# A graph network's recurrent kernel: tiles 4 to 7 prepared every four units with their state split in two pieces, masking moved to GpSimd, last chain in halves

## Chip, cores and metric

The kernel runs on one core of a Trainium2 chip. The metric is the device time of one execution in microseconds; lower is better.

## What is computed

```python
h = relu(layernorm(x))                       # x: 64 graphs, 128 nodes, 128 channels
A = (adj != 0)
for l in range(5):
    m   = einsum('bnd,de->bne', h, weight[l])
    agg = einsum('bij,bid->bjd', A, m)
    # GRU cell:
    gi, gh = agg @ w_ih.T + b_ih, h @ w_hh.T + b_hh
    r, z = sigmoid(i_r + h_r), sigmoid(i_z + h_z)
    n = tanh(i_n + r * h_n)
    h = (1 - z) * n + z * h
return x + h * mask[..., None]
```

## The kernel before

The 64 graphs make 16 tiles of four graphs, 128 channels by 512 node columns. The tiles go in four groups of four. Within a group the five layers run one after another, and within a layer the four tiles. A pair (tile, layer) is a **unit**; there are N = 80, numbered K = 0 to 79: tiles 0 to 3 have units 0 to 19, tiles 4 to 7 units 20 to 39, and so on, so unit K + 4 is the next layer of unit K's tile. Every product is made of three float16 matmuls from high and low halves (`three`, L293 to L295).

**One unit.** TensorE makes three products from the old state, `ps_r`, `ps_z`, `ps_hn` (`h_products`), then two from the aggregated state s, then the `aggregate` of the *next* unit into `ps_s` (eight narrow matmuls, L366 and L367), then `ps_in` from s. ScalarE makes r (L478), z (L484), the high half of s (L472), the high half of the previous unit's state (`state_high`, L494) and n (L488). VectorE makes r * hn (L624), the input of tanh (L630), the low half of s of the next unit (`s_low`, L618), and the new state in two steps (L636, L641). GpSimd makes z * h (`kept`, L816) and the low half of the previous unit's state (`state_low`, L821). SyncE then issues `transpose(K)` (L242), a DMA that turns both halves into `nat`; `aggregate(K + 4)` waits for it.

**Preparation.** Each tile from 4 on passes through stages beside the units of earlier tiles. `prep[t]` is the unit of stage 0, set in L54 to L57 by counting back from the tile's first unit with a distance of 3 units (tiles 4 to 7) or 5. Stage 0: loads of adj and x on SyncE, `moments` on VectorE. Stage 1: `aggregate` of the moments on VectorE, `inverse_std` on GpSimd. Stages 3 and 4: `layernorm` in halves on ScalarE (L442). Stage 5: `natural_high` (ScalarE) and `natural_low` (GpSimd, L804). Stage 6: `split` on ScalarE (L467), then two DMA transposes, `transpose_first` and `transpose_halves`; for tiles below 8 also `adjacency` on GpSimd (L800). Stage 7: `adjacency` on VectorE (L609) for the later tiles. Stages 8 and 9: `join` in halves on VectorE (L676). `STAGES` is their number.

**Results.** A finished tile is masked (`masked_result`, L827) in the unit `ends[t]`, added to x (`final`, L835) in the next, and stored by SyncE in the one after (`storing`). `fetching` says when `load_ends` brings the x and mask rows of a tile, six units ahead of `ends`; the mask row is broadcast to 128 partitions. In the last group, units 76 to 78, VectorE multiplies by the mask itself (`masked_state`, L648). The last unit has a chain of its own: `masked_open`, `last_result`.

**What sets the order.** Each engine runs a loop over K with the calls written out by hand, and takes them strictly in that order; so does SyncE with its DMA issues, all on one queue. In SyncE's loop, iteration K has `transpose(K - 1)`, the loads of stage 0, the transposes of stage 6, the store and the fetch, in this order.

```python
prep[t] = min(at[t, 0] - STAGES, prep[t + 1] - gap if t + 1 < TILES else N)
ends[t] += (prep[TILES - 1] + 3 - ends[t]) % SPREAD
```

Of the kernel before, what the change touches and what calls it, by code (L numbers as in the profile page):

```python
# [27 lines left out]
FINISH = 3  # L28
STAGES = 10
# [7 lines left out]
def gnn_kernel(nc, x, xT, adj, mask_row, fold_lhs, w_ihT, w_hhT, bias_ih, bias_hh, ident, out):  # L37
# [10 lines left out]
    END = at[starts[-1], LAST]  # L48
# [33 lines left out]
    with ExitStack() as ctx:  # L82
# [66 lines left out]
        ps_s, ps_t, ps_f = bank("ps_s"), bank("ps_t"), bank("ps_f")  # L149

# [31 lines left out]
        def block_of(tile_ap, q):  # L182
            return tile_ap[:, q * P:(q + 1) * P]

# [30 lines left out]
        def _(sp):  # L215
# [16 lines left out]
            def transpose_halves(t):  # L232
                sp.wait_ge(split_done, t - FIRST + 1)
# [39 lines left out]
            for K in range(1, N + 2):  # L273
# [6 lines left out]
                if K in tile_at_stage[6]:  # L280
                    transpose_first(tile_at_stage[6][K])
                    transpose_halves(tile_at_stage[6][K])
                if K in storing:
                    store(storing[K])
                for t in fetching.get(K, ()):
                    load_ends(t)
            for f in range(FRING):
                sp.wait_ge(stored[f], 16 * len(range(f, TILES, FRING)))
# [146 lines left out]
        def _(act):  # L435
# [26 lines left out]
            def split(t):  # L462

                act.wait_ge(h0_done, 2 * t + 2)
                if t - FIRST >= 2:
                    act.wait_ge(halves_loaded[t % 2], 16 * ((t - FIRST) // 2))
                nc.scalar.copy(halves[:, t % 2], h0[:, t % LN].bitcast(U16).rearrange("p (c b) -> p b c", b=2)).then_inc(  # L467
                    split_done, 1)
# [11 lines left out]
            def gate_z(K):  # L480
# [3 lines left out]
                nc.scalar.activation(z[:, K % 2], ps_z[:], ACT.Sigmoid, bias=b_sum[:, 1:2], scale=unscale[:, 0:1]).then_inc(z_done, 1)  # L484

# [14 lines left out]
            def move_mask():  # L500
# [3 lines left out]
                act.wait_ge(s_lo_done, N)  # L504
                nc.scalar.copy(ps_s[:], mask_in[:, f]).then_inc(mask_moved, 1)

            def store_last():
                t = TILES - 1
                act.wait_ge(last_out, 1)
                act.dma_start(out_t[t], x_out[:, t % FRING]).then_inc(stored[t % FRING], 16)  # L510
# [30 lines left out]
            for K in range(N):  # L541
# [16 lines left out]
                if K == 0:  # L558
                    layernorm(3, 0)
                    layernorm(3, 1)  # L560
                else:
                    gate_n(K)
# [19 lines left out]
        def _(dve):  # L582
# [67 lines left out]
            def masked_open(K):  # L650
# [5 lines left out]
                nc.vector.scalar_tensor_tensor(out=mask_in[:, f], in0=z[:, K % 2], scalar=1.0, in1=ps_s[:],  # L656
                                               op0=ALU.subtract, op1=ALU.mult).then_inc(open_done, 1)

            def last_result(K):

                f = units[K][0] % FRING
                dve.wait_ge(n_done, K + 1)
                dve.wait_ge(open_done, 1)
                nc.vector.tensor_tensor(ps_in[K % 2][:], mask_in[:, f], ps_in[K % 2][:], ALU.mult).then_inc(zn_done, 1)
                dve.wait_ge(zn_done, K + 1)
                dve.wait_ge(last_kept, 1)
                nc.vector.tensor_tensor(x_out[:, f], x_out[:, f], ps_in[K % 2][:], ALU.subtract).then_inc(last_out, 1)
# [79 lines left out]
            for K in range(N):  # L747
# [8 lines left out]
                if K in tile_at_stage[0]:  # L756
                    moments(tile_at_stage[0][K])
# [164 lines left out]
```

## Time and profile before

| | |
|---|---|
| time, median of 3 runs | 371.98 us (371.85 to 372.28) |
| the profiled execution's own time | 371.11 us |
| its span, first to last instruction | 369.2 us |
| TensorE matmul | 360.0 us busy, 98% |
| VectorE | 322.8 us, 87% |
| ScalarE | 299.8 us, 81% |
| GpSimd | 263.6 us, 71% |
| mean granted TensorE clock | 0.997 of 2.4 GHz |
| packets of SyncE's DMA queue | 45.37 MB, 55.3% of the time of 16 DMA engines |
| chain of work that ended last | TensorE 90%, VectorE 4%, DMA 2%, GpSimd 2% |

The page's busy shares are averages. The timeline of an engine gives each instruction's start, its length and, in brackets, how long the engine had been idle and for whom. Durations of neighbours overlap by about 0.1 us, since an engine begins an instruction before its predecessor has fully ended.

### The profile page before, as it was taken

The numbers are of one execution on the slowest core, as the hardware profiler recorded it, in microseconds if no ns is written. First come the engines' busy times: TensorE is split into PE (matmuls) and PEld (weight loads), VectorE is DVE, ScalarE is ACT, GpSimd is POOL, SyncE is SP. The second block draws the span as 40 slices with busy tenths as digits, with TensorE's granted clock in tenths as the row PEclk, the third lists the DMA queues.
The fourth block names the chain that finished last, engine by engine and source line by source line (L and its number), as shares of the span: only waits on it lengthen the run. The fifth ranks groups of instructions, "written<-read, shape, count | busy, mean of one in ns | idle before, by whom it ended". The sixth has DMA issues, their size and how long they took to land.

```text
span 369.2 us, 6528 instructions
## 1 busy us (share of the span) xinstructions
PE 360.0 (98%) x2125; PEld 181.1 (49%) x2125; DVE 322.8 (87%) x588; ACT 299.8 (81%) x495; POOL 263.6 (71%) x261
## 2 busy tenths in 40 slices
PE   7999999999999999999999999999999999999992
PEld 3455555544454555555545455555545555555541
DVE  4977898899889999999999999999998988787886
ACT  5997788998879988888877889899877767777753
POOL 3765758889578878787656878888756777755574
PEclk9999999999999999999999999999999999999998
DMA  8634443857662693939624384756834543349522
GB/s 245 211 59 86 115 97 76 170 126 151 152 115 45 147 180 78 228 68 200 169 42 105 64 197 85 164 123 158 151 94 112 130 99 59 89 100 231 124 57 85
DMA packets 108512, 46.03 MB, mean 125 GB/s; under 512 B 97728, under 2 KB 98112, under 8 KB 108480
## 3 DMA queue, kind: packets, MB, share of 16 engines
q1 hardware_dynamic: 108336, 45.37, 55.3%
q8 instruction: 17, 0.28, 0.3%
q10 hardware_dynamic: 144, 0.26, 0.2%
q14 instruction: 15, 0.12, 0.1%
HBM read 17.57 MB, written 4.19 MB: 59 GB/s over the span
## 4 chain that ended last, share of the span: by engine, by line
PE 90%; DVE 4%; DMA 2%; POOL 2%; issue 1%; ACT 1%; DVEq 0%; POOLq 0%
PE ps_r L293 9%; PE ps_z L294 9%; PE ps_z L293 9%; PE ps_r L294 9%; PE ps_z L295 9%; PE ps_r L295 9%; PE ps_s L366 5%; PE ps_s L367 5%; PE ps_in L295 4%; PE ps_hn L294 4%; PE ps_in L293 4%; PE ps_in L294 4%; PE ps_hn L295 4%; PE ps_hn L293 4%; DMA hp<-nat 1%
## 5 line engine op out<-in xcount | busy, mean ns | idle before, releaser
L816 POOL TENSOR_TENSOR zh<-z,h 128x512 f32<-128x512 f32 x80 | 101.9, 1273 | 81.4 <-ACT z L484 81.3
L478 ACT ACTIVATE r<-ps_r,b_sum,unscale 128x512 f32<-128x512 f32 x80 | 62.2, 778 | 37.9 <-PE ps_r L295 37.5
L488 ACT ACTIVATE ps_in<-ps_in,b_ih,unscale 128x512 f32<-128x512 f32 x80 | 60.1, 751 | 22.3 <-DVE ps_in L630 21.3
L821 POOL TENSOR_TENSOR hp<-h,hp 128x512 f16<-128x512 f32 x64 | 74.1, 1157 | 0.0
L624 DVE SCALAR_TENSOR_TENSOR rhn<-ps_hn,b_hn,r 128x512 f32<-128x512 f32 x80 | 59.8, 748 | 10.3 <-ACT r L478 9.8
L630 DVE TENSOR_TENSOR ps_in<-ps_in,rhn 128x512 f32<-128x512 f32 x80 | 56.0, 700 | 11.5 <-PE ps_in L295 6.7
L484 ACT ACTIVATE z<-ps_z,b_sum,unscale 128x512 f32<-128x512 f32 x80 | 61.6, 770 | 0.7 <-PE ps_z L295 0.7
L641 DVE TENSOR_TENSOR h<-zh,ps_in 128x512 f32<-128x512 f32 x76 | 52.2, 687 | 8.5 <-DVE ps_in L636 0.5
L636 DVE SCALAR_TENSOR_TENSOR ps_in<-z,ps_in 128x512 f32<-128x512 f32 x79 | 54.7, 692 | 5.6 <-ACT ps_in L488 5.6
L618 DVE TENSOR_TENSOR s_lo<-ps_s,s_hi 128x512 f16<-128x512 f32 x80 | 54.4, 680 | 0.4 <-ACT s_hi L472 0.4
L472 ACT CAST s_hi<-ps_s 128x512 f16<-128x512 f32 x80 | 46.6, 583 | 0.0
L366 PE MATMUL ps_s<-a,nat 128*128 128x128 f16 x320 | 44.3, 219 | 0.0
L367 PE MATMUL ps_s<-a,nat 128*128 128x128 f16 x320 | 44.3, 219 | 0.0
L494 ACT CAST hp<-h 128x512 f16<-128x512 f32 x64 | 40.7, 635 | 0.1
L366 PEld LDWEIGHTS ps_s<-a,nat 128*128 128x128 f16 x320 | 31.3, 98 | 9.4 <-POOL nat L804 0.4
L367 PEld LDWEIGHTS ps_s<-a,nat 128*128 128x128 f16 x320 | 31.3, 98 | 9.0
L293 PE MATMUL ps_z<-s_hi,v_hi 128*128 128x512 f16 x80 | 30.3, 379 | 0.5 <-DVE s_lo L618 0.5
L293 PE MATMUL ps_r<-s_hi,v_hi 128*128 128x512 f16 x80 | 30.4, 380 | 0.2 <-DVE s_lo L618 0.2
L293 PE MATMUL ps_r<-hp,u_hi 128*128 128x512 f16 x79 | 30.0, 379 | 0.5 <-DMA hp<-nat 0.2
L294 PE MATMUL ps_r<-s_lo,v_hi 128*128 128x512 f16 x80 | 30.3, 379 | 0.0
L295 PE MATMUL ps_r<-s_hi,v_lo 128*128 128x512 f16 x80 | 30.3, 379 | 0.0
L294 PE MATMUL ps_z<-s_lo,v_hi 128*128 128x512 f16 x80 | 30.3, 379 | 0.0
(115 smaller groups left out, 745.0 us busy)
## 6 DMA issues: line engine op xcount, KB each, us to landing
x_in<-in_x SPq DMA_DIRECT2D x16, 256.0 KB, 3.8
adj_in<-in_adj SPq DMA_DIRECT2D x16, 256.0 KB, 3.4
x_out<-in_xT SPq DMA_DIRECT2D x16, 256.0 KB, 3.1
mask_in<-in_mask_row SPq DMA_DIRECT2D x16, 256.0 KB, 3.8
out<-x_out SPq DMA_DIRECT2D x15, 256.0 KB, 2.7
nat<-hp SPq DMA_TRANSPOSE x64, 3.1
fold_in<-in_fold_lhs SPq DMA_DIRECT2D x1, 320.0 KB, 3.9
out<-x_out ACTq DMA_DIRECT2D x1, 256.0 KB, 2.1
```

The source lines that it names most:

```text
L293: nc.tensor.matmul(ps[:], w_hi, m_hi, start=start, stop=False)
L294: nc.tensor.matmul(ps[:], w_hi, m_lo, start=False, stop=False)
L295: return nc.tensor.matmul(ps[:], w_lo, m_hi, start=False, stop=stop)
L366: nc.tensor.matmul(block_of(ps_s, q), block_of(nat_hi(t), q), a_q, start=True, stop=False)
L367: last = nc.tensor.matmul(block_of(ps_s, q), block_of(nat_lo(t), q), a_q, start=False, stop=True)
L478: nc.scalar.activation(r[:], ps_r[:], ACT.Sigmoid, bias=b_sum[:, 0:1], scale=unscale[:, 0:1]).then_inc(r_done, 1)
L484: nc.scalar.activation(z[:, K % 2], ps_z[:], ACT.Sigmoid, bias=b_sum[:, 1:2], scale=unscale[:, 0:1]).then_inc(z_done, 1)
L488: nc.scalar.activation(ps_in[K % 2][:], ps_in[K % 2][:], ACT.Tanh, bias=b_ih[:, 2:3], scale=unscale[:, 0:1]).then_inc(n_done, 1)
L624: nc.vector.scalar_tensor_tensor(out=rhn[:], in0=ps_hn[:], scalar=b_hn[:, 0:1], in1=r[:], op0=ALU.add, op1=ALU.mult).then_inc(rhn_done, 1)
L630: nc.vector.tensor_tensor(ps_in[K % 2][:], ps_in[K % 2][:], rhn[:], ALU.add).then_inc(npre_done, 1)
L816: nc.gpsimd.tensor_tensor(zh[:, K % 2], z[:, K % 2], h[:, t % RING], ALU.mult).then_inc(zh_done, 1)
L821: nc.gpsimd.tensor_tensor(h_lo(t), h[:, t % RING], h_hi(t), ALU.subtract).then_inc(h_lo_done, 1)
```

## The change

Five things are changed.

- Tiles 4 to 7 follow each other by four units and not three. `prep` becomes 2, 6, 10, 14 for tiles 4 to 7 (it was 4, 7, 10, 13) and 19, 24, ... 54 for tiles 8 to 15 (it was 18, 23, ... 53).
- There are nine stages. `layernorm` stands in stages 2 and 3, `natural_high`, `natural_low` and the first half of `split` in 4, its second half, the two transposes and GpSimd's `adjacency` in 5, VectorE's `adjacency` in 6, `join` in 7 and 8. `moments` of tiles 4 to 7 come two units ahead of stage 0.
- Since `ends` is aligned to `prep`, the stores move too: from units 23, 28, ... 58 to 19, 24, ... 59, and the fetches from 15, 20, ... 50 to 11, 16, ... 51; `load_ends(9)` falls in unit 54.
- `END` is 78: units 76 and 77 write their state like all others, and GpSimd masks it ahead of the next unit's `kept`. The last tile's old state is masked one unit earlier, and its mask is copied to PSUM ahead of the last z.
- In unit 79, tanh and the two operations behind it run in halves of 256 columns, and each half is stored by itself, the first by SyncE, the second by ScalarE's queue.

The core of the diff:

```diff
-FINISH = 3
-STAGES = 10
+FINISH = 4
+STAGES = 9
...
-    END = at[starts[-1], LAST]
+    END = N - 1 - 1
...
-        gap = 3 if t < starts[1] + GROUPS[1] else SPREAD
+        gap = 4 if t < starts[2] else SPREAD
...
+    measured = {prep[t] - (2 if t < starts[2] else 0): t for t in prep}
...
+        last_n = (ps_f, ps_s)
...
-                if K in tile_at_stage[6]:
-                    transpose_first(tile_at_stage[6][K])
-                    transpose_halves(tile_at_stage[6][K])
+                if K in tile_at_stage[5]:
+                    transpose_first(tile_at_stage[5][K])
+                    transpose_halves(tile_at_stage[5][K])
...
+            sp.wait_ge(last_out, 1)
+            sp.dma_start(half_of(out_t[TILES - 1], 0), half_of(x_out[:, (TILES - 1) % FRING], 0)).then_inc(
+                stored[(TILES - 1) % FRING], 16)
...
-            def split(t):
-
-                act.wait_ge(h0_done, 2 * t + 2)
+            def split(t, half):
+
+                act.wait_ge(h0_done, 2 * t + 1 + half)
...
+            def last_gate_n(K, half):
+                act.wait_ge(npre_done, K + 1)
+                nc.scalar.activation(last_n[half][:, 0:TILE // 2], half_of(ps_in[K % 2], half), ACT.Tanh, bias=b_ih[:, 2:3],
+                                     scale=unscale[:, 0:1]).then_inc(n_done, 1)
...
                 else:
+                    move_mask()
                     gate_z(K)
                     gate_r(K)
-                    move_mask()
...
+                if K in tile_at_stage[2]:
+                    layernorm(tile_at_stage[2][K], 0)
                 if K in tile_at_stage[3]:
-                    layernorm(tile_at_stage[3][K], 0)
+                    layernorm(tile_at_stage[3][K], 1)
                 if K in tile_at_stage[4]:
-                    layernorm(tile_at_stage[4][K], 1)
+                    natural_high(tile_at_stage[4][K])
+                if K in tile_at_stage[4]:
+                    split(tile_at_stage[4][K], 0)
                 if K in tile_at_stage[5]:
-                    natural_high(tile_at_stage[5][K])
-                if K in tile_at_stage[6]:
-                    split(tile_at_stage[6][K])
+                    split(tile_at_stage[5][K], 1)
...
-                if K in tile_at_stage[0]:
-                    moments(tile_at_stage[0][K])
+                if K in measured:
+                    moments(measured[K])
...
                     masked_open(K)
-                    last_result(K)
+                    last_open_n(K, 0)
+                    last_open_n(K, 1)
+                    last_result(K, 0)
+                    last_result(K, 1)
...
             for K in range(N):
+                if END > K - 1 >= at[starts[-1], LAST]:
+                    masked_result(units[K - 1][0])
                 kept(K)
...
-                if K in tile_at_stage[5]:
-                    natural_low(tile_at_stage[5][K])
-                if K in tile_at_stage[6] and pool_compares(tile_at_stage[6][K]):
-                    adjacency(tile_at_stage[6][K])
+                if K in tile_at_stage[4]:
+                    natural_low(tile_at_stage[4][K])
+                if K in tile_at_stage[5] and pool_compares(tile_at_stage[5][K]):
+                    adjacency(tile_at_stage[5][K])
```

SyncE's queue around units 23 to 25, before. `nat<-hp` is a unit's state transpose, `hp<-nat` and `halves_t<-halves` are the transposes of a tile in preparation, `out_0<-x_out` is a store; the last two rows are a fetch.

```order
43 L242 DMA_TRANSPOSE nat<-hp 128x8x128 x3
44 L224 DMA adj_in<-in_adj 128x512
45 L219 DMA x_in<-in_x 128x512
46 L253 DMA out_0<-x_out 128x512
47 L242 DMA_TRANSPOSE nat<-hp 128x8x128
48 L230 DMA_TRANSPOSE hp<-nat 128x8x128
49 L236 DMA_TRANSPOSE halves_t<-halves 128x8x128
50 L242 DMA_TRANSPOSE nat<-hp 128x8x128
51 L248 DMA x_out<-in_xT 128x512
52 L249 DMA mask_in<-in_mask_row 128x512
```

The same place after the change.

```order
49 L248 DMA_TRANSPOSE nat<-hp 128x8x128 x3
50 L230 DMA adj_in<-in_adj 128x512
51 L225 DMA x_in<-in_x 128x512
52 L236 DMA_TRANSPOSE hp<-nat 128x8x128
53 L242 DMA_TRANSPOSE halves_t<-halves 128x8x128
54 L259 DMA out_0<-x_out 128x512
55 L248 DMA_TRANSPOSE nat<-hp 128x8x128 x2
56 L254 DMA x_out<-in_xT 128x512
57 L255 DMA mask_in<-in_mask_row 128x512
```

The loads, the two preparing transposes and the store stand between two neighbouring state transposes, where a state transpose used to divide them into two turns. The fetch has moved back by one.

GpSimd's last operations before, from the last `state_low` on (`L841` masks the last tile's old state, `L835` adds, `L847` is the last tile's share of z * h).

```order
252 L821 TENSOR_TENSOR hp<-h,hp 128x512
253 L816 TENSOR_TENSOR zh<-z,h 128x512
254 L841 TENSOR_TENSOR h<-mask_in,h 128x512
255 L835 TENSOR_TENSOR x_out<-x_out,mask_in 128x512
256 L816 TENSOR_TENSOR zh<-z,h 128x512
257 L835 TENSOR_TENSOR x_out<-x_out,mask_in 128x512
258 L816 TENSOR_TENSOR zh<-z,h 128x512
259 L847 TENSOR_TENSOR x_out<-x_out,zh 128x512
260 L835 TENSOR_TENSOR x_out<-x_out,mask_in 128x512
```

And after; `L854` is the masking that has come from VectorE.

```order
253 L848 TENSOR_TENSOR hp<-h,hp 128x512
254 L868 TENSOR_TENSOR h<-mask_in,h 128x512
255 L854 TENSOR_TENSOR mask_in<-mask_in,h 128x512
256 L843 TENSOR_TENSOR zh<-z,h 128x512
257 L862 TENSOR_TENSOR x_out<-x_out,mask_in 128x512
258 L854 TENSOR_TENSOR mask_in<-mask_in,h 128x512
259 L843 TENSOR_TENSOR zh<-z,h 128x512
260 L862 TENSOR_TENSOR x_out<-x_out,mask_in 128x512
261 L843 TENSOR_TENSOR zh<-z,h 128x512
262 L874 TENSOR_TENSOR x_out<-x_out,zh 128x512
263 L862 TENSOR_TENSOR x_out<-x_out,mask_in 128x512
```

The masking of the last old state comes ahead of unit 77's `zh`, and each of the two new maskings stands in front of a `zh`.

## Rows read from the trace of the kernel before

**Rows 1.** The page: engines; DMA issues with median us to landing.
```profile
PE 360.0 (98%) x2125; PEld 181.1 (49%) x2125; DVE 322.8 (87%) x588; ACT 299.8 (81%) x495; POOL 263.6 (71%) x261
...
nat<-hp SPq DMA_TRANSPOSE x64, 3.1
```

**Rows 2.** Timeline, GpSimd, unit 25: start us, us, engine, line, operation, out<-in.
```profile
129.87 1.16 POOL L821 TENSOR_TENSOR hp<-h,hp 128x512 f16<-128x512 f32 x1
```

**Rows 3.** Timeline, TensorE: the first matmul of two neighbouring aggregations.
```profile
131.89 0.22 PE L366 MATMUL ps_s<-a,nat 128*128 128x128 f16 x1
...
136.22 0.22 PE L366 MATMUL ps_s<-a,nat 128*128 128x128 f16 x1
```

**Rows 4.** Timeline, ScalarE: a split.
```profile
78.43 1.03 ACT L467 COPY halves<-h 128x1024 uint16<-128x1024 uint16 x1
```

**Rows 5.** Timeline, TensorE's weight loads; brackets: idle before, released by.
```profile
80.26 0.10 PEld L293 LDWEIGHTS ps_r<-hp,u_hi 128*128 128x128 f16 x1 [0.59 <-issue]
...
82.40 0.10 PEld L293 LDWEIGHTS ps_r<-s_hi,v_hi 128*128 128x128 f16 x1 [0.51 <-DVE s_lo L618]
```

**Rows 6.** Timeline, VectorE: an aggregate, a join, and an adjacency.
```profile
104.31 0.37 DVE L597 BATCH_NORM_AGGREGATE mean_var<-bn 128x2 f32<-128x6 f32 x4
104.60 0.42 DVE L676 COPY h<-halves_t 128x512 uint16<-128x512 uint16 x1
...
130.06 1.25 DVE L609 TENSOR_SCALAR a<-adj_in 128x512 f16<-128x512 f32 x1
```

**Rows 7.** Timeline, GpSimd: an adjacency, then natural_low and the next zh.
```profile
77.99 1.93 POOL L800 TENSOR_SCALAR a<-adj_in 128x512 f16<-128x512 f32 x1
...
122.60 1.16 POOL L804 TENSOR_TENSOR nat<-h,nat 128x512 f16<-128x512 f32 x1 [0.24 <-ACT nat L450]
124.31 1.27 POOL L816 TENSOR_TENSOR zh<-z,h 128x512 f32<-128x512 f32 x1 [0.54 <-ACT z L484]
```

**Rows 8.** Timeline, SyncE's queue: the issue of unit 23's transpose.
```profile
126.73 1.30 SPq L242 DMA_TRANSPOSE nat<-hp  x1
```

**Rows 9.** Timeline, SyncE's queue from 79.3 us: issues.
```profile
79.33 0.58 SPq L224 DMA_DIRECT2D adj_in<-in_adj  x1
79.95 0.43 SPq L219 DMA_DIRECT2D x_in<-in_x  x1
...
83.43 1.78 SPq L242 DMA_TRANSPOSE nat<-hp  x1
```

**Rows 10.** DMA issues from 79.3 to 83.6 us: us from issue to landing.
```profile
adj_in<-in_adj SPq DMA_DIRECT2D x1, 256.0 KB, 3.1
x_in<-in_x SPq DMA_DIRECT2D x1, 256.0 KB, 3.4
...
nat<-hp SPq DMA_TRANSPOSE x1, 3.7
```

**Rows 11.** Timeline, SyncE's queue from 254.2 us: issues.
```profile
254.26 0.44 SPq L253 DMA_DIRECT2D out<-x_out  x1
254.75 0.44 SPq L248 DMA_DIRECT2D x_out<-in_xT  x1
255.23 0.50 SPq L249 DMA_DIRECT2D mask_in<-in_mask_row  x1
```

**Rows 12.** DMA issues from 254.2 to 255.6 us: us from issue to landing.
```profile
out<-x_out SPq DMA_DIRECT2D x1, 256.0 KB, 3.4
x_out<-in_xT SPq DMA_DIRECT2D x1, 256.0 KB, 3.6
mask_in<-in_mask_row SPq DMA_DIRECT2D x1, 256.0 KB, 4.8
```

**Rows 13.** Timeline near the end: masking, the last unit's first s-product, last operations.
```profile
357.51 0.69 DVE L648 TENSOR_TENSOR mask_in<-mask_in,ps_in 128x512 f32<-128x512 f32 x1
...
360.31 0.39 PE L293 MATMUL ps_z<-s_hi,v_hi 128*128 128x512 f16 x1 [0.53 <-DVE s_lo L618]
...
365.05 0.69 DVE L664 TENSOR_TENSOR ps_in<-mask_in,ps_in 128x512 f32<-128x512 f32 x1 [0.23 <-ACT ps_in L488]
```

More of the change, by code:

```diff
@@ L183, in block_of, with half_of @@
             return tile_ap[:, q * P:(q + 1) * P]
+        def half_of(tile_ap, half):
+            return tile_ap[:, half * TILE // 2:(half + 1) * TILE // 2]
         def h_hi(t):
@@ L460, in transposed @@
                 nc.scalar.activation(h[:, t % RING], ps_t[:], ACT.Relu).then_inc(h_init, 1)
-            def split(t):
-                act.wait_ge(h0_done, 2 * t + 2)
+            def split(t, half):
+                act.wait_ge(h0_done, 2 * t + 1 + half)
                 if t - FIRST >= 2:
                     act.wait_ge(halves_loaded[t % 2], 16 * ((t - FIRST) // 2))
-                nc.scalar.copy(halves[:, t % 2], h0[:, t % LN].bitcast(U16).rearrange("p (c b) -> p b c", b=2)).then_inc(
-                    split_done, 1)
+                nc.scalar.copy(halves[:, t % 2, :, half * TILE // 2:(half + 1) * TILE // 2],
+                               h0[:, t % LN, half * TILE // 2:(half + 1) * TILE // 2].bitcast(U16).rearrange(
+                                   "p (c b) -> p b c", b=2)).then_inc(split_done, 1)
             def s_high(K):
@@ L503, in move_mask @@
                 act.wait_ge(ends_loaded[f], 32 * ((TILES - 1) // FRING + 1))
-                act.wait_ge(s_lo_done, N)
-                nc.scalar.copy(ps_s[:], mask_in[:, f]).then_inc(mask_moved, 1)
+                nc.scalar.copy(ps_t[:], mask_in[:, f]).then_inc(mask_moved, 1)
             def store_last():
                 t = TILES - 1
-                act.wait_ge(last_out, 1)
-                act.dma_start(out_t[t], x_out[:, t % FRING]).then_inc(stored[t % FRING], 16)
+                act.wait_ge(last_out, 2)
+                act.dma_start(half_of(out_t[t], 1), half_of(x_out[:, t % FRING], 1)).then_inc(stored[t % FRING], 16)
             def squares(weights, begin, sums):
@@ L655, in masked_open, with last_open_n, last_result @@
                 dve.wait_ge(mask_moved, 1)
-                nc.vector.scalar_tensor_tensor(out=mask_in[:, f], in0=z[:, K % 2], scalar=1.0, in1=ps_s[:],
+                nc.vector.scalar_tensor_tensor(out=mask_in[:, f], in0=z[:, K % 2], scalar=1.0, in1=ps_t[:],
                                                op0=ALU.subtract, op1=ALU.mult).then_inc(open_done, 1)
-            def last_result(K):
-                f = units[K][0] % FRING
-                dve.wait_ge(n_done, K + 1)
+            def last_open_n(K, half):
+                dve.wait_ge(n_done, K + 1 + half)
                 dve.wait_ge(open_done, 1)
-                nc.vector.tensor_tensor(ps_in[K % 2][:], mask_in[:, f], ps_in[K % 2][:], ALU.mult).then_inc(zn_done, 1)
-                dve.wait_ge(zn_done, K + 1)
+                n = last_n[half][:, 0:TILE // 2]
+                nc.vector.tensor_tensor(n, half_of(mask_in[:, units[K][0] % FRING], half), n, ALU.mult).then_inc(zn_done, 1)
+            def last_result(K, half):
+                dve.wait_ge(zn_done, K + 1 + half)
                 dve.wait_ge(last_kept, 1)
-                nc.vector.tensor_tensor(x_out[:, f], x_out[:, f], ps_in[K % 2][:], ALU.subtract).then_inc(last_out, 1)
+                result = half_of(x_out[:, units[K][0] % FRING], half)
+                nc.vector.tensor_tensor(result, result, last_n[half][:, 0:TILE // 2], ALU.subtract).then_inc(last_out, 1)
             def join(t, half):
@@ L755, in _ @@
                     adjacency(3)
-                if K in tile_at_stage[0]:
-                    moments(tile_at_stage[0][K])
+                if K in measured:
+                    moments(measured[K])
                 if K in tile_at_stage[1]:
                     aggregate(tile_at_stage[1][K])
-                if K in tile_at_stage[7] and not pool_compares(tile_at_stage[7][K]):
-                    adjacency(tile_at_stage[7][K])
+                if K in tile_at_stage[6] and not pool_compares(tile_at_stage[6][K]):
+                    adjacency(tile_at_stage[6][K])
                 for half in range(2):
-                    if K in tile_at_stage[8 + half]:
-                        join(tile_at_stage[8 + half][K], half)
+                    if K in tile_at_stage[7 + half]:
+                        join(tile_at_stage[7 + half][K], half)
                 if K == 0:
@@ L830, in final @@
                 f = t % FRING
-                if t < starts[-1]:
+                if at[t, LAST] < END:
                     pool.wait_ge(masked, t + 1)
                 else:
-                    pool.wait_ge(last_masked, t - starts[-1] + 1)
+                    pool.wait_ge(last_masked, at[t, LAST] - END + 1)
                 nc.gpsimd.tensor_tensor(x_out[:, f], x_out[:, f], mask_in[:, f], ALU.add).then_inc(out_done, 1)
```

9 lines of the change are left out of this document (6 added, 3 removed).

## The prediction

> **What bounds the kernel now.** I read the page's engine line first: TensorE is busy 360.0 of 369.2 us [rows 1]. A kernel like this gains only where TensorE's stream of matmuls has a hole, and loses only where a new hole opens. In the steady part the aggregations of neighbouring units start 4.33 us apart [rows 3], which is 18 wide matmuls and 8 narrow ones back to back. So the second view was the timeline of TensorE, searched for starts that follow their predecessor by more than the usual 0.22 us. From 27 to 359 us it found only a fold of weights, two pairs of short holes and one crumb, all before 97 us. The third view was the timeline of the other engines around these, the fourth the queue of DMA issues with the time to landing of each. From 97 to 359 us the stream has no hole. That stretch can't get faster; it can only be hurt.
>
> Where it could be hurt is read from slack. The state's `transpose` of a unit K is issued when GpSimd has written the low half (L821) in unit K+1, and its result is wanted by `aggregate(K+4)`. For K = 24 GpSimd ends at 129.87 + 1.16 = 131.03; the aggregation starts at 136.22 [rows 2, 3]. So **a transpose has 5.2 us from "ready" to "wanted"**. Undisturbed it lands 3.1 us after its issue [rows 1], and 2.1 us are spare.
>
> **Part 1: preparation of tiles 4 to 7, and the split in pieces.** Before, tiles 4 to 7 follow each other by three units, and a tile's `split` (stage 6) shares a unit with the next tile's first `layernorm` (stage 3). ScalarE then has a split of 1.03 us from 78.43 behind a half layernorm [rows 4], and the next r, whose sum was ready near 78.4, gets its turn when that is through, 0.9 us late. TensorE pays: the weights of the next unit are loaded after 0.59 us of idleness and those of its s-products after 0.51 us [rows 5]; start to start, the matmuls lose 0.29 and 0.18 us. The pair comes back three units later with 0.28 and 0.14, and one hole of 0.07 lies between. Sum: 0.96. With tiles four units apart and stages 2, 3, 4, 5 on ScalarE, no unit has two tiles' work; the fullest has `natural_high` and half a split. Half a split I take at 0.55, between 0.4 and 1.03 [rows 4]. That is 1.2 us where about 0.8 is free; r is 0.4 late, and the first hole needed r 0.9 late. Gain: **-1.0** (bounds -1.1 and -0.6, if VectorE's joins, up to 1.3 us in units 13 and 14, leave a crumb). The early `moments(4)` in unit 0 fills a wait of VectorE for `v_hi`; zero.
>
> Moments and aggregate of tiles 8 to 15 come one unit later. `aggregate` (0.37 us, of which 0.3 are its turn [rows 6]) now stands ahead of `adjacency` on VectorE in seven units (25, 30, ... 55). Added to a 1.25 us adjacency [rows 6] it would make s_lo 0.3 late, seven times. But a join lasted 0.42 us at 104.60, while GpSimd had only 4-column work, and the adjacency at 130.06 lasted 1.25 and ended at 131.31, 0.28 after GpSimd's L821 ended [rows 2, 6]. It is a wait, not work, and 0.3 more ahead of it disappears in it. I take 0, and keep 7 x 0.3 = 2.1 as a bound. The Trainium skill (SBUF — State Buffer, "Who interferes with whom") says the pair of ports that VectorE's two-port modes share with GpSimd is an exclusive lock for a whole instruction; by that rule the sum has 0 here, by adding durations 2.1.
>
> **Part 2: what moves on SyncE's queue.** This is the term that decides. Before, in each period of five units, loads and the store stand in one unit (23), `transpose_first` and `transpose_halves` in the next (24), the fetch in the third (25). After, stage 0 of one tile, stage 5 of the tile before and the store all fall on the same unit: 24, 29, 34, 39, 44, 49, 54. Between the transposes of units 23 and 24 then stand adjacency load, x load, two transposes and a store; before, only the two transposes. On top of that GpSimd has `natural_low` and `final` in one unit (23, 28, ...): natural_low ends near 123.75 [rows 7], final takes at least 1.27, as zh does, so the next zh starts at 125.0, not at 124.31, and the transpose of unit 23 is issued at 127.4, not at 126.73 [rows 7, 8].
>
> The price comes from the one place of before that has almost this queue, SyncE's turn from 79.33 us on: adjacency and x load, first, halves, state transpose. The adjacency load was issued at 79.33, the transpose at 83.43, and it landed 3.7 us later, at 87.13 [rows 9, 10]: **7.8 us after the adjacency load's issue**. In the new unit 24 that load is issued 1.3 after the transpose, at 128.7. The transpose of unit 24 would land at 136.5; with a store ahead of it too, later by one 256 KB copy. Landings lie 0.7 apart there (254.26 + 3.4 against 254.75 + 3.6) [rows 11, 12]. So 137.2 against 136.2: TensorE waits **1.0** in unit 27, likewise after units 29 and 34. Bounds: 0 (without the 0.7 of GpSimd and with the store free, 135.8) and 1.9 (issue at 133.3, landing 4.8, the longest shown [rows 12]).
> - Units 24, 29, 34: 3 x 1.0 = **+3.0** (0 to 5.7). Unit 39 is a last layer and has no transpose.
> - Units 44, 49: no x load, 0.9 less (79.33 + 3.1 against 79.95 + 3.4 [rows 9, 10]): 2 x 0.1 = **+0.2** (0 to 2.0).
> - Unit 54: `load_ends(9)` stands behind the store as well: 0.7 for x_out, and 1.7 for the mask row (254.75 + 3.6 = 258.35 against 255.23 + 4.8 = 260.03 [rows 11, 12]): 0.1 + 2.4 = **+2.5** (0 to 3.5).
> - Unit 11: GpSimd has `inverse_std` (1.7, three small operations around a 1.0 us power) and an `adjacency` of 1.93 [rows 7] in the same unit: with zh and L821 6.1 us in 4.33, so its next handover is 1.7 late and leaves 0.4 of the 2.1. Alone that fits (units 7, 15). In unit 11 the fetch for tile 0, with its mask row, now goes ahead of the transpose: **+0.6** (0 to 1.2), a hole near `aggregate(15)`.
>
> A wait in `aggregate` shifts everything behind it, so the holes add. Halves land near 135.1 where the join wants them at 134.7, but the join waits for L821 until 135.3 anyway: nothing.
>
> **Part 3: the end.** Masking of tiles 12 and 13 leaves VectorE (0.69 at 357.51) for GpSimd. VectorE is what the last unit waits for: the first `ps_z<-s_hi,v_hi` of unit 79 starts at 360.31 after 0.53 us of waiting for s_lo [rows 13]. Most of that goes: -0.5. On GpSimd, masked_last_h (unit 76), masked_result and zh follow each other; zh of unit 77 ends near 355.7, wanted at 356.4. Thin, but enough. The last chain (tanh, then two operations of VectorE, 0.69 each [rows 13]) in halves gains about 0.3 by overlap and pays that for four more issues and for `masked_open`, which now ends later than the first half of tanh. The store of 256 KB in two halves lets the first leave sooner: -0.1. The Trainium skill (DMA: Bandwidth & Descriptors, "Rules for kernel authors") advises against splitting a transfer in partition halves, since both use the same 16 engines; read onto these halves by column it would make this 0.1 a 0. Sum: **-0.6** (-1.0 to -0.1).
>
> **Sum**: -1.0 - 0.6 + 3.0 + 0.2 + 2.5 + 0.6 = +4.7. The profiled execution took 371.11, so 375.8 there; it lies 0.87 below the median of the runs, 371.98, and on that the forecast is **376.7 us**.
>
> **The rivals.** A measurement tells a change from none here at about 0.2%, 0.74 us.
> - *The queue swallows it, and the change does what it says.* Every transpose lands within 5.2 us of being ready. Then only the gains stand: 371.98 - 1.6 = 370.4. For it: 2.1 us of slack is much, the longest landing of before did no harm, and the overshoot of 1.0 is built from a template plus 0.7 for GpSimd and 0.7 for the store. It decides at the landing of unit 24's transpose, 136.2 on before's clock: with 1.0 us less of the delays that I add up, the three middle holes close. Against it: the template alone already ends at 136.5. Chance 0.24.
> - *Only unit 54 overflows*, where the mask row goes ahead: +2.5 - 1.6 = +0.9, 372.9. Chance 0.14, half of it within 0.2%.
> - *VectorE becomes the bound in units 25 to 55*: the 0.3 adds up after all, +2.1 - 1.6 = +0.5, 372.5, without holes from DMA. The two ends that follow L821 speak against it. Chance 0.05, mostly within 0.2%.
> - *The forecast*: several holes of TensorE, 374.5 to 379.5. Chance 0.57.
>
> **How the numbers follow.** Slower by over 0.2%: 0.57 + 0.07 + 0.02 = 0.66. Same: 0.10. Faster: 0.24. The range takes in the fast rival at its likeliest, 370.3, and goes up to 379.5, where two of the DMA terms sit at their upper bounds; the sum of all upper bounds would be above 382, and I leave that out.
>
> **What would show it.** Right: TensorE's holes at 80, 82, 93 and 96 us gone; new waits of `ps_s` matmuls or their weight loads (L366) for a DMA `nat<-hp`, in units 27, 32, 37 and, the longest, 57; transposes in units 25, 30, 35, 55 issued 1.5 to 3 us after GpSimd's low half and landing in 3.7 us or more; GpSimd's zh late by 0.7 in units 24, 29. The last product ends about 0.6 us earlier than before, both measured from the start of unit 76. Wrong: TensorE without a hole from 97 us on, and SyncE's transposes landing before 5.2 us are up; or holes released by s_lo, which would make VectorE the cause.

## The result, and the profile after

| | before | after |
|---|---|---|
| time, median | 372.13 us (371.76 to 372.46, 6 runs) | 374.75 us (374.02 to 375.31, 6 runs) |
| ratio after / before, 95% interval | | 1.007 (1.0056 to 1.0084) |
| the profiled execution's own time | 371.11 us | 374.98 us |
| its span | 369.2 us | 373.0 us |

The change makes the kernel slower by 2.6 us. The forecast was 376.7 us and slower, so its direction was right; it had +4.7 us where +2.6 were measured. The page of the changed kernel, its engine line and the aggregation's two groups (busy us, mean ns, idle time ahead and its releaser):

```profile
PE 360.8 (97%) x2125; PEld 181.6 (49%) x2125; DVE 320.0 (86%) x588; ACT 301.5 (81%) x508; POOL 264.3 (71%) x263
...
PE 68%; POOL 10%; DMA 6%; SPq 5%; DVE 5%; issue 3%; ACT 2%; DVEq 0%; POOLq 0%
...
L375 PE MATMUL ps_s<-a,nat 128*128 128x128 f16 x320 | 44.4, 219 | 3.9 <-DMA nat<-hp 3.9
...
L375 PEld LDWEIGHTS ps_s<-a,nat 128*128 128x128 f16 x320 | 31.1, 98 | 15.3 <-DMA nat<-hp 6.7
```

The busy times are those of [rows 1] within 3 us. What is new is in the chain: TensorE had 90% of it, now DMA, SyncE's queue and GpSimd have 21% between them. The two groups name the place: `aggregate` waits for the state transpose `nat<-hp`, which it never did from 97 us on before. The list of waits confirms it (us in total, times, longest), and shows that VectorE is not the cause: the weight loads that wait for s_lo, those of the s-products, did so for 9.3 us before, in 34 places, and now for 5.2 us in 20.

```profile
PEld ps_s L375 <- DMA nat<-hp: 6.7, 7, 2.2
...
PEld ps_r L302 <- DVE s_lo L638: 5.2, 20, 0.8
...
PE ps_s L375 <- DMA nat<-hp: 3.9, 4, 1.7
```

The timeline of TensorE in four of the units that wait:

```profile
79.90 0.23 PE L375 MATMUL ps_s<-a,nat 128*128 128x128 f16 x1 [0.36 <-DMA nat<-hp]
...
137.54 0.23 PE L375 MATMUL ps_s<-a,nat 128*128 128x128 f16 x1 [1.14 <-DMA nat<-hp]
...
160.06 0.23 PE L375 MATMUL ps_s<-a,nat 128*128 128x128 f16 x1 [0.69 <-DMA nat<-hp]
...
270.41 0.23 PE L375 MATMUL ps_s<-a,nat 128*128 128x128 f16 x1 [1.66 <-DMA nat<-hp]
```

These are units 14, 27, 32 and 57. A fifth, unit 37, has a hole too short for a bracket. The bracket holds the idle time; what the stream loses is the distance of two starts less the usual one: 0.52, 1.30, 0.85, 0.21 (unit 37) and 1.83, in sum **4.71 us**. The five small holes of before at 80 to 96 us (0.96) are gone.

Now the queue that delays unit 24's transpose. Timeline of SyncE in the changed kernel, from the issue of unit 23's transpose on:

```profile
127.37 1.23 SPq L248 DMA_TRANSPOSE nat<-hp  x1
128.65 0.58 SPq L230 DMA_DIRECT2D adj_in<-in_adj  x1
129.28 0.43 SPq L225 DMA_DIRECT2D x_in<-in_x  x1
129.76 1.24 SPq L236 DMA_TRANSPOSE hp<-nat  x1
131.09 1.72 SPq L242 DMA_TRANSPOSE halves_t<-halves  x1
132.88 0.87 SPq L259 DMA_DIRECT2D out<-x_out  x1
133.79 1.28 SPq L248 DMA_TRANSPOSE nat<-hp  x1
```

GpSimd in the units ahead of it:

```profile
122.61 1.16 POOL L831 TENSOR_TENSOR nat<-h,nat 128x512 f16<-128x512 f32 x1 [0.24 <-ACT nat L459]
123.72 1.28 POOL L862 TENSOR_TENSOR x_out<-x_out,mask_in 128x512 f32<-128x512 f32 x1
124.95 1.28 POOL L843 TENSOR_TENSOR zh<-z,h 128x512 f32<-128x512 f32 x1
126.18 1.17 POOL L848 TENSOR_TENSOR hp<-h,hp 128x512 f16<-128x512 f32 x1
...
129.88 1.15 POOL L848 TENSOR_TENSOR hp<-h,hp 128x512 f16<-128x512 f32 x1
```

And the DMA issues from 133.7 to 134.9 us, with us from issue to landing:

```profile
out<-x_out SPq DMA_DIRECT2D x1, 256.0 KB, 3.7
nat<-hp SPq DMA_TRANSPOSE x1, 3.7
```

Read together: `final` (L862) behind `natural_low` (L831) puts zh at 124.95 where it was at 124.31 [rows 7], so unit 23's transpose leaves at 127.37 and not at 126.73 [rows 8]. The five issues behind it then hold the queue until 133.79. GpSimd had unit 24's low half ready at 129.88 + 1.15 = 131.03, exactly when before [rows 2]. The transpose left 2.8 us later, took 3.7, landed at 137.49, and TensorE started at 137.54. The prediction had an issue near 133.3 to 133.5 and a landing at 137.2.

In unit 54 the fetch of tile 9 stands in the same turn (SyncE's queue, then landings of the DMAs issued from 265.4 to 266.5 us):

```profile
264.35 0.59 SPq L259 DMA_DIRECT2D out<-x_out  x1
264.99 0.44 SPq L254 DMA_DIRECT2D x_out<-in_xT  x1
265.47 0.46 SPq L255 DMA_DIRECT2D mask_in<-in_mask_row  x1
```

```profile
mask_in<-in_mask_row SPq DMA_DIRECT2D x1, 256.0 KB, 3.8
nat<-hp SPq DMA_TRANSPOSE x1, 4.4
```

The transpose follows at 265.97, 1.0 us later for the two issues of the fetch, needs 4.4 and lands at 270.4, where `aggregate` starts at 270.41. In unit 11 it is `x_out` (73.90) and the mask row (74.64) that stand ahead. Both issues are over 0.7 us before GpSimd has the low half ready, so the transpose leaves at 75.84 in any case; but it takes 4.0 us, and opens the hole at 79.90.

**The balance of the two profiled spans** is +3.8: holes +4.71, holes of before -0.96, a head that is 0.49 longer in this execution (the first full unit starts at 27.84 and not at 27.35; in the profiles of all the other kernels here it lies from 27.5 to 28.3, so it is not put down to the change), and -0.4 at the end. The profiled execution of before was among its shortest, 0.9 below the first median; that of after lay 0.2 above its own. So 3.9 us between profiles are 2.6 us between medians. Without the head, the first profile of after would still make it 3.3; the changed kernel's second profile, further below, has 4.2 us of holes, which makes it 2.9, as its ratio does.

### The profile page after: what moved, and what is told of

It reads as the page before. It is cut to its first block, busy times and chain, and to the rows that moved or that the text cites. A ratio compares the mean times of both kernels' runs of the same rounds, so it can differ in the third digit from the quotient of the medians.

```text
span 373.0 us, 6555 instructions
## 1 busy us (share of the span) xinstructions
PE 360.8 (97%) x2125; PEld 181.6 (49%) x2125; DVE 320.0 (86%) x588; ACT 301.5 (81%) x508; POOL 264.3 (71%) x263
## 4 chain that ended last, share of the span: by engine, by line
PE 68%; POOL 10%; DMA 6%; SPq 5%; DVE 5%; issue 3%; ACT 2%; DVEq 0%; POOLq 0%
PE ps_r L302 7%; PE ps_z L304 7%; PE ps_r L304 7%; PE ps_z L302 7%; PE ps_z L303 7%; PE ps_r L303 7%; DMA nat<-hp 4%; PE ps_s L375 4%; PE ps_s L376 4%; PE ps_in L304 3%; PE ps_in L303 3%; PE ps_in L302 3%; PE ps_hn L302 3%; PE ps_hn L304 3%; PE ps_hn L303 3%
## 5 line engine op out<-in xcount | busy, mean ns | idle before, releaser
L503 ACT ACTIVATE ps_in<-ps_in,b_ih,unscale 128x512 f32<-128x512 f32 x79 | 59.3, 750 | 17.8 <-DVE ps_in L650 16.5
L661 DVE TENSOR_TENSOR h<-zh,ps_in 128x512 f32<-128x512 f32 x78 | 53.6, 687 | 9.2 <-POOL zh L843 0.9
L304 PE MATMUL ps_z<-s_hi,v_lo 128*128 128x512 f16 x80 | 30.3, 379 | 0.0
```

The source lines that it names most:

```text
L304: return nc.tensor.matmul(ps[:], w_lo, m_hi, start=False, stop=stop)
L503: nc.scalar.activation(ps_in[K % 2][:], ps_in[K % 2][:], ACT.Tanh, bias=b_ih[:, 2:3], scale=unscale[:, 0:1]).then_inc(n_done, 1)
```

## Experiments

Three accounts of the 2.6 us were open. **Queue**: loads, preparing transposes and store between two state transposes delay the second past its 2.1 us of slack. **GpSimd**: the queue would be bearable, `final` beside `natural_low` starts it 0.7 too late. **Rest**: something else in the new stages. Time differences between variants are taken from their ratios to before (371.56 to 371.68 in these comparisons; the changed kernel's are 1.0070 and, repeated, 1.0077, so +2.6 to +2.9 us). They can differ from the quotients of the medians by up to 0.0007, 0.3 us. Start-to-start excess of TensorE at `aggregate`, us, from one profiled execution each:

| kernel | unit 14 | 18 | 27 | 32 | 37 | 57 | time, ratio to before |
|---|---|---|---|---|---|---|---|
| after | 0.52 | 0 | 1.30 | 0.85 | 0.21 | 1.83 | 1.0070 |
| after again | 0.79 | 0 | 1.18 | 0 | 0.19 | 2.05 | 1.0077 |
| results where they were | 0 | 1.16 | 0.50 | 0 | 0 | 0 | 1.0004 |
| loads early | 0.57 | 0 | 0 | 0 | 0 | 1.66 | 1.0006 |
| final late | 0 | 0 | 1.08 | 0 | 0 | 1.47 | 1.0060 |
| store late | 0.11 | 0 | 0.85 | 0 | 0 | 1.53 | 1.0019 |
| fetch late | 0 | 0 | 1.37 | 0.14 | 0.90 | 0 | 1.0026 |
| before, packed | 0 | 0 | 0.91 | 0 | 0.12 | 0 | 1.0034 |
| loads early, fetch late | 0 | 0 | 0 | 0 | 0 | 0 | 0.9949 |

For unit 24's transpose, whose hole is the one in unit 27, the same profiles give how long after GpSimd's low half it was issued and how long it then took. Their sum less the 5.2 us of room is the hole, within 0.1 in every row:

| kernel | issued after ready | issue to landing | sum less 5.2 | hole in unit 27 |
|---|---|---|---|---|
| after | 2.8 | 3.7 | 1.3 | 1.30 |
| after again | 2.5 | 3.8 | 1.1 | 1.18 |
| fetch late | 2.7 | 3.8 | 1.3 | 1.37 |
| before, packed | 2.3 | 3.8 | 0.9 | 0.91 |
| final late | 2.2 | 4.0 | 1.0 | 1.08 |
| store late | 1.8 | 4.3 | 0.9 | 0.85 |
| results where they were | 1.2 | 4.5 | 0.5 | 0.50 |
| loads early | 1.0 | 3.6 | none | 0 |
| loads early, fetch late | 1.0 | 3.3 | none | 0 |

As long as both loads stay in the turn, a transpose that leaves earlier lands after a longer time, so about half of the lead is lost again.

One column can't be trusted singly. The edits of "final late" and "store late" change nothing before unit 18, and yet the hole of unit 14 is 0 and 0.11 there: in the five profiles with a fetch ahead of it, unit 11's transpose took 3.3 to 4.3 us to land.

### Results, stores and fetches where before had them

```diff
-            ends[t] += (prep[TILES - 1] + 3 - ends[t]) % SPREAD
+            ends[t] += (prep[TILES - 1] + 2 - ends[t]) % SPREAD
```

> The changed kernel with masking, adding, storing and fetching of the tiles one unit back in each period (ends aligned to prep + 2), as they stood before; preparation and end stay as changed. Queue theory (what stands between two neighbouring state transposes on SyncE, together with GpSimd's natural_low and final in one unit, opens TensorE's holes): the holes in units 14, 27, 32, 37 and 57, 4.7 us in all, go to under 0.1 each, and the time falls to about 1.3 us under the kernel before, 370.8. Rival (the preparation itself is dearer: late moments, split in two pieces): the time stays over 373.

Measured: 371.73 us against 371.56, ratio 1.0004 (0.9987 to 1.0021). About 2.5 us of the loss go, but the expected gain of before's holes does not come. The timeline of TensorE shows two holes, one of them new:

```profile
97.62 0.23 PE L375 MATMUL ps_s<-a,nat 128*128 128x128 f16 x1 [1.00 <-DMA nat<-hp]
...
137.12 0.23 PE L375 MATMUL ps_s<-a,nat 128*128 128x128 f16 x1 [0.34 <-DMA nat<-hp]
```

Its cause, in the timelines of GpSimd and of SyncE's queue ahead of unit 18, and in the landings there:

```profile
88.78 1.94 POOL L827 TENSOR_SCALAR a<-adj_in 128x512 f16<-128x512 f32 x1
90.69 1.27 POOL L843 TENSOR_TENSOR zh<-z,h 128x512 f32<-128x512 f32 x1
91.92 1.16 POOL L848 TENSOR_TENSOR hp<-h,hp 128x512 f16<-128x512 f32 x1
```

```profile
91.62 0.58 SPq L254 DMA_DIRECT2D x_out<-in_xT  x1
92.24 0.43 SPq L255 DMA_DIRECT2D mask_in<-in_mask_row  x1
93.11 1.24 SPq L248 DMA_TRANSPOSE nat<-hp  x1
```

```profile
nat<-hp SPq DMA_TRANSPOSE x1, 4.5
```

Moving the results back put the fetch, with its mask row, from unit 11 into unit 15, where GpSimd again has `inverse_std` and `adjacency` in one unit. That is the mechanism the prediction priced for unit 11, met at its next place. The second hole shows that without the store, too, the loads and two transposes are too much: unit 24's transpose leaves at 132.62, only 1.2 us after its low half, but needs 4.5 us to land. The queue is confirmed, and moving a transfer alone is no cure.

### Loads one unit earlier

```diff
+    loading = {prep[t] - (t >= starts[2]): t for t in prep}
...
-                if K in tile_at_stage[0]:
-                    load_adj(tile_at_stage[0][K])
+                t = loading.get(K)
+                if t is not None:
+                    load_adj(t)
```

(`load_x` moves with it.)

> The changed kernel with only the loads of stage 0 of tiles 8 to 15 issued one unit earlier (23, 28, ...), so that two transposes and a store alone stand between the state transposes of units 23 and 24. Queue theory: that transpose is issued 1.0 us earlier and has two copies less ahead of it; the holes in units 27, 32, 37 (1.30, 0.85, 0.21) go to 0, the one in unit 57 from 1.83 to about 1.0 (one load less), the one in unit 14 (0.52) stays; the time falls by about 3 us. Rival (GpSimd's late handover alone opens the holes): holes of 27 and 32 keep more than half their size.

Measured: 371.91, ratio 1.0006 (0.9993 to 1.0018). The holes of units 27, 32 and 37 are gone and those of 14 and 57 stay, as a cause in the queue demands. The time falls by 2.4 to 2.6 us. Unit 57 gave back 0.2 to 0.4 where 0.8 was expected: only the adjacency load moves out there, and the fetch still stands ahead of the transpose.

### GpSimd's final one unit later

```diff
-    adding = {adds[t]: t for t in ends if t < TILES - 2}
+    adding = {adds[t] + (t < starts[2]): t for t in ends if t < TILES - 2}
```

> The changed kernel with GpSimd's final of tiles 0 to 7 one unit later, in the store's own unit, so that natural_low and final no longer share a unit; SyncE's queue has the same order. If GpSimd's 0.65 us of lateness passes on in full, as the sum had it, the holes shrink by 0.65 each: 1.30 to 0.65 in unit 27, 0.85 to 0.2 in 32, 0.21 to 0 in 37, 1.83 to 1.2 in 57, and the time falls by about 2.1 us. If the queue alone decides, they stay as they are.

Measured: 373.53 (4 runs), ratio 1.006 (1.0045 to 1.0075). SyncE's order is untouched. Unit 27's hole is still 1.08. By the ratios 0.4 to 0.6 us are gained and the intervals overlap with the changed kernel's; by the quotients of the medians it would be 0.7 to 1.1. This profile's holes, unit 14 left out, are 0.9 to 1.6 us less than those of the two profiles of after, but it is the fastest of its four runs. So neither "in full" (2.1) nor "they stay as they are" holds, and how much GpSimd's lateness costs stays open between 0.4 and 1.6 us. In unit 24 the transpose leaves 0.3 to 0.5 us earlier after its low half, but lands after 4.0 us and not 3.7 or 3.8, which takes back half or more.

### The store one unit later

```diff
-    storing = {adds[t] + 1: t for t in ends}
+    storing = {adds[t] + 1 + (t < starts[2]): t for t in ends}
```

> The changed kernel with only the stores of tiles 0 to 7 one unit later (25, 30, ...), behind the state transpose they stood ahead of. Queue theory: the transpose is issued 0.9 us earlier and has one copy less ahead, so 0.7 to 0.9 off each hole: 27 to about 0.5, 32 to about 0.1, 37 to 0, 57 to about 1.0; time down by about 2.3 us. Rival (a store, writing to memory, doesn't hold up transposes inside the chip): less than 0.3 off each.

Measured: 371.99, ratio 1.0019 (1.0002 to 1.0037): 1.9 to 2.2 us back. The holes of units 32 and 37 are gone, those of 27 and 57 shrink by 0.3 to 0.5 (expected: 0.7 to 0.9): the transpose of unit 24 does leave earlier, but takes 4.3 us. A store is not free, but it costs less than the queue theory had it.

### The fetch one unit later

```diff
-    fetching = {ends[t] - FETCH: [t] for t in ends}
+    fetching = {ends[t] - FETCH + (t < starts[-1]): [t] for t in ends}
```

> The changed kernel with only the fetches of tiles 0 to 11 one unit later (12, 17, ... 52, 55, ...). Queue theory: the holes that need a mask row ahead of the state transpose go: unit 14 from 0.52 to 0 and unit 57 from 1.83 to about 0.1; those in units 27, 32 and 37 stay (2.4 in all). Time down by about 2.2 us. Rival (GpSimd's inverse_std with adjacency opens the hole of unit 14): that hole stays.

Measured: 372.60, ratio 1.0026 (1.0014 to 1.0039): 1.6 to 1.9 us back. The holes of units 14 and 57 are gone, the middle ones stay (2.4 us in all, unit 27: 1.37). So each of the two groups has its own cause, as the prediction had it. For unit 57 this is clear: 1.47 to 2.05 in the five profiles with the fetch ahead, 0 in the three of after's variants without. Unit 14's hole is too unsteady for one profile to decide, but unit 11's transpose landed after 3.1 us in all three profiles without a fetch ahead and never under 3.3 with one.

The four parts, undone one at a time, give back about 2.5, 0.5, 2.0 and 1.7 us, more than the 4.2 to 4.7 us of holes that there are. A threshold explains it: a transpose has 2.1 us to spare, and one transfer less brings several of the crowded turns below it at once.

### Before, with only its queue packed

The opposite test: the kernel before, with nothing of the change but the order on SyncE's queue. Tiles 8 and on are loaded, and tiles 0 to 7 stored, one unit later, so that both fall in the turn of the preparing transposes. GpSimd's work stays where it was.

```diff
+    loading = {prep[t] + (t >= starts[2]): t for t in prep}
...
-    storing = {adds[t] + 1: t for t in ends}
+    storing = {adds[t] + 1 + (t < starts[2]): t for t in ends}
```

> The kernel before, with loads of tiles 8 to 15 and stores of tiles 0 to 7 one unit later. Units 24, 29, ... then have on SyncE the very order of the changed kernel (two loads, two transposes, store, state transpose), while GpSimd and all else stay as before. Queue theory: holes from DMA open in units 27, 32 and 37, of about 0.3 to 0.6 each since GpSimd's 0.65 us isn't there; the time is 372.1 + 0.9 to 1.8 us. Rival (GpSimd's lateness is needed): no hole, 372.1.

Measured: 372.70 against 371.62, ratio 1.0034 (1.0018 to 1.0051), so +1.3 us. The timeline of SyncE's queue of this kernel, and its `aggregate` of unit 27:

```profile
127.28 1.23 SPq L243 DMA_TRANSPOSE nat<-hp  x1
128.55 0.58 SPq L225 DMA_DIRECT2D adj_in<-in_adj  x1
129.17 0.44 SPq L220 DMA_DIRECT2D x_in<-in_x  x1
129.66 1.23 SPq L231 DMA_TRANSPOSE hp<-nat  x1
130.99 2.21 SPq L237 DMA_TRANSPOSE halves_t<-halves  x1
133.25 0.58 SPq L254 DMA_DIRECT2D out<-x_out  x1
133.87 1.30 SPq L243 DMA_TRANSPOSE nat<-hp  x1
```

```profile
137.69 0.23 PE L368 MATMUL ps_s<-a,nat 128*128 128x128 f16 x1 [0.75 <-DMA nat<-hp]
```

The five issues between two state transposes open the hole of unit 27, 0.91 of its 1.2 to 1.4 us, in a kernel in which no aggregation waited for a transpose otherwise, and with GpSimd on time. Cause shown, from both sides. The expected three holes of 0.3 to 0.6 came as one large and one of 0.12, though the turns are alike; the total fits. Most of the lateness is the five issues themselves. Some is added where an issue takes longer: `halves_t<-halves` needs 2.21 us here and 1.72 in the changed kernel, against 1.3 in quiet turns, but also 1.28 in the changed kernel's repetition.

### Only the end

The kernel before with `END` = 78, the mask in PSUM ahead of the last z, and the last chain and store in halves; preparation and queue as before.

```diff
-    END = at[starts[-1], LAST]
+    END = N - 1 - 1
...
-                    last_result(K)
+                    last_open_n(K, 0)
+                    last_open_n(K, 1)
+                    last_result(K, 0)
+                    last_result(K, 1)
```

> The kernel before with only the end of the change: tiles 12 and 13 masked on GpSimd, last chain and last store in halves; preparation, results and SyncE's queue as before. By the sum -0.6 us; by the two traces the last VectorE operation ends 0.6 earlier but the store lands 0.2 later behind it, so -0.4: 371.7.

Measured: 371.51 against 371.62, ratio 0.9998 (0.9987 to 1.001): -0.1, with 0.4 to either side. The trace of this kernel has the predicted shape (the last unit's hole 0.20 instead of 0.69), but a gain of 0.6 lies outside the interval's lower end of about -0.5.

### A kernel without the crowded turns

Loads early and fetch late together: the change, with its preparation and end, but no turn of SyncE that holds all of it.

> The changed kernel with both: loads of tiles 8 to 15 one unit earlier and fetches of tiles 0 to 11 one unit later. Queue theory: no state transpose has more than two transposes and one store ahead of it, so all five holes from DMA are gone (under 0.3 us in sum) while the holes at 80, 82, 93 and 96 us stay closed. Time: before 371.6, less 1.0 for these, less 0 to 0.4 for the end: 370.2 to 370.6, faster than both kernels. Rival (the packed preparation costs TensorE or VectorE something else, or the DMA holes only move, as one did to unit 18 in the first experiment): 371.3 or more.

Measured: **369.80** (369.31 to 370.37) against 371.68, ratio **0.9949** (0.9936 to 0.9962). It beats before by 1.9 us and the changed kernel by 4.9, and lies 0.4 below the expected 370.2 to 370.6. The list of waits, and the turn of unit 24 on SyncE's queue:

```profile
PEld ps_s L377 <- DMA nat<-hp: 0.2, 1, 0.2
```

```profile
126.68 1.24 SPq L249 DMA_TRANSPOSE nat<-hp  x1
127.96 1.35 SPq L237 DMA_TRANSPOSE hp<-nat  x1
129.41 1.29 SPq L243 DMA_TRANSPOSE halves_t<-halves  x1
130.75 0.57 SPq L260 DMA_DIRECT2D out<-x_out  x1
```

Unit 24's transpose is issued at 131.37, 1.0 us after its low half where the changed kernel has 2.8, and lands after 3.3 us, at 134.7. TensorE has no hole left that a DMA makes, and those of the preparation are gone as well. Of the 1.9 us the traces account for 1.1 between the profiled spans (368.1 against 369.2: holes of the preparation -0.96, last unit -0.5, head +0.3). Why the medians stand 0.8 further apart is open; the single times of before spread over 1.8 us (371.13 to 372.94) and this kernel's over 1.1, so before may lose something in part of its executions that its one profile does not show.

### The same, with the last store whole

```diff
-            sp.dma_start(half_of(out_t[TILES - 1], 0), half_of(x_out[:, (TILES - 1) % FRING], 0)).then_inc(
-                stored[(TILES - 1) % FRING], 16)
...
-                act.dma_start(half_of(out_t[t], 1), half_of(x_out[:, t % FRING], 1)).then_inc(stored[t % FRING], 16)
+                act.dma_start(out_t[t], x_out[:, t % FRING]).then_inc(stored[t % FRING], 16)
```

> The kernel of the previous line, with the last tile's store whole, issued by ScalarE after both halves, as before the change; the arithmetic of the last chain stays in halves. If two half stores land 0.2 us later than one whole, as the two profiled executions suggest (2.92 against 2.73 us from the last VectorE operation's end to the span's end), this is 0.2 us faster; if the half that leaves first helps, as the sum had it, 0.1 slower. Either is at the edge of what the runs can tell, and the trace's last stretch decides.

Measured: 370.16, ratio 0.9956 (0.9944 to 0.9968), not to be told from the kernel with halves. Landings of the last stores, first that kernel, then this one:

```profile
out<-x_out SPq DMA_DIRECT2D x1, 128.0 KB, 2.0
out<-x_out ACTq DMA_DIRECT2D x1, 128.0 KB, 2.3
```

```profile
out<-x_out ACTq DMA_DIRECT2D x1, 256.0 KB, 2.2
```

Half the bytes take the same time, and the end comes 2.88 and 2.87 us after VectorE's last operation ends. In these traces the split store is worth 0; the times can't tell 0 from 0.1.

### The changed kernel once more

It was run unaltered beside the last two, to see how far single holes repeat.

> The changed kernel unaltered, beside the two above on the same chip, to see how much its holes vary from one execution to the next. Five holes of 4.7 us in sum in its first profile; expected again holes in units 27, 32 or 37 and in 57, 3.5 to 5 us in sum with single ones differing by up to 0.5, and 374.3 to 374.8 us.

Measured: 374.72, ratio 1.0077 (1.006 to 1.0095). The sum of the holes is 4.2 us against 4.7, but unit 32 has none this time and unit 57 has 2.05. Sums of holes can be compared between profiles to about 0.5 us; a single hole differs by up to 0.9 us, where 0.5 was expected.

## Why the prediction was right, and where it was not

- **Where the kernel is bound, and what it could lose.** Right. TensorE is busy for 360 us in both, and all of the loss is in holes of the stream. The slack of 5.2 us from ready to wanted, 2.1 of it to spare, decided.
- **Part 1, the preparation, -1.0.** Right: five holes with 0.96 us are gone in the trace, and ScalarE's halves of `split` take 0.60 where 0.55 was taken. Its worth by itself was not timed.
- **VectorE's aggregate ahead of adjacency, 0 against 2.1.** Right. Timeline of VectorE in the changed kernel, unit 25:

```profile
130.07 0.37 DVE L617 BATCH_NORM_AGGREGATE mean_var<-bn 128x2 f32<-128x6 f32 x4
130.36 0.95 DVE L629 TENSOR_SCALAR a<-adj_in 128x512 f16<-128x512 f32 x1
```

  The adjacency starts 0.3 later, lasts 0.95 instead of 1.25, and ends at 131.31, on the hundredth where it ended before [rows 6], 0.28 after GpSimd's low half. In unit 40, where there is no low half to write and GpSimd has at most 4-column work, the same operation of this kernel takes 0.39:

```profile
197.73 0.39 DVE L629 TENSOR_SCALAR a<-adj_in 128x512 f16<-128x512 f32 x1
```

  So the rest was a wait for GpSimd. The Trainium skill (SBUF — State Buffer, "Who interferes with whom") has the shared pair of ports as an exclusive lock for a whole instruction; the trace agrees.
- **Units 24, 29 and 34, 3 x 1.0.** The mechanism was right, and for unit 24 the sizes too: issue and landing at 133.79 and 137.49 where the sum has 133.3 to 133.5 and 137.2. The holes are 1.30, 0.85 and 0.21, sum 2.36, and 1.37 in the repetition. The step that failed is the multiplication: the term was worked out for unit 24 and taken for all. The three turns have the same five issues, but the transposes of units 29 and 34 leave 1.9 and 2.2 us after their low halves, not 2.8, and land after 4.1 and 3.2 us; in the repetition unit 29's also takes 3.2, and the hole is gone. One reason shows in the trace: GpSimd's low half of units 28 and 33 is 0.35 us late and not 0.65. Why the landing varies by 0.9 us in one and the same turn is open. The term is oversized by 0.6 us of the 1.6 by which all holes together were missed, and in the repetition by 1.6 of 2.1.
- **Units 44 and 49, +0.2.** Measured 0.
- **Unit 54, +2.5.** Measured 1.83 and 2.05. The mask row landed 3.8 us after its issue and not 4.8 [rows 12], so its price was probably too high; that this alone made the 0.5 to 0.7 us of difference isn't shown.
- **Unit 11, +0.6.** Measured 0.52 and 0.79. That this is so near is in part luck: the same hole was 0.57, 0.11 and 0 in three variants that leave it untouched. That the same would happen in unit 15 if a fetch came there was shown by the first experiment.
- **GpSimd 0.7 late.** The delay itself is there within 0.05 us in unit 23 (124.95 and 127.37 for 125.0 and 127.4), but taking it away gave back 0.4 to 0.6 us in all by the ratios, and shortened unit 27's hole by 0.1 to 0.3, not by 0.7 in each turn.
- **Part 3, the end, -0.6.** In the trace -0.4, timed alone -0.1 with 0.4 to either side. The halves are as fast as thought (tanh 0.54 and 0.53, VectorE 0.43 and 0.41), and the last product comes 0.5 us earlier, but the time behind VectorE's last operation is 2.9 us where it was 2.7, and the store brings nothing. The rule of the Trainium skill (DMA: Bandwidth & Descriptors, "Rules for kernel authors") against splitting a transfer in partition halves, read onto halves by column, has 0 for that tenth; the landings above agree, the times can't tell.
- **The sum.** 376.7 was forecast and 374.75 measured, 1.95 less, while the direction and the mechanism held. Predicted holes 6.3 us, measured 4.7 and 4.2. In the profiled execution, with its head 0.5 longer and 0.2 less gained at the end, that makes 374.98 for 375.8, 0.8 of the miss. The other 1.1 lies in the step from one profile to the median: 0.87 was added for both kernels, as if the median of after would lie above its profiled execution by as much, and it lay 0.2 below.
- **The rivals.** "The queue swallows it" and "only unit 54 overflows" fell at unit 27's hole, 1.30 us at 137.54. "VectorE becomes the bound" fell at the waits for s_lo, which are fewer than before.

## What to carry to other kernels

Before the phase of a software pipeline is changed, write down for every period what will stand on each queue between two transfers that somebody waits for, and compare the last one's landing with the slack from ready to wanted: here five issues fitted into two turns and not into one. Align what shares a queue, not what belongs to one tile, and put bulk loads, stores and broadcast rows in turns of their own; two lines of the schedule that did so turned +2.6 us into -1.9. While the loads stayed ahead of the transpose, issuing it earlier gave back only about half of the lead; taking the loads out of the turn closed the holes. When a cost is worked out for one of several like places, don't take it in full for all: the same five issues cost 1.3, 0.9 and 0.2 us here.

## What was not expected of the hardware

- The landing time of a transpose depends on what was issued ahead of it. Undisturbed it is 3.1 to 3.3 us. Behind the packed turn of unit 24 it is 3.7 to 4.0 with the store, 4.3 and 4.5 without it, when the transpose itself leaves earlier; 4.4 and 4.7 behind a mask row in unit 54, 4.5 where a fetch stood ahead of it (issued at 93.11), 3.3 to 4.3 in unit 11.
- Issuing, too, can take longer in the packed turn: 1.24 us for one transpose in quiet turns, 1.72 and 2.21 in the packed one, 0.57 for a copy and 0.87 in the packed one. In the repetition of the changed kernel the same transpose took 1.28 and the store 1.03.
- At the end of the kernel, a store of 128 KB from a column half lands after 2.0 to 2.3 us, one of 256 KB after 2.2.
- The head of the kernel, up to the first full unit, varies by up to 0.9 us between the profiles, as much as several of the effects looked for here.
